# A decoder layer on one core: what opens TensorE's work, and who computes the last layer norm's mean and variance

## What is computed

```python
x = layernorm(x + self_attention(x))             # 16 heads of 64, causal
x = layernorm(x + cross_attention(x, ctx, mask)) # 16 heads of 8, with biases
# feed-forward: 8 experts of width 256, two of them weighted per token
for e in range(8):
    h = silu(x @ w_gate[e].T) * (x @ w_up[e].T)
    out = out + dense_w[:, e:e + 1] * (h @ w_down[e].T)
x = layernorm(x + out)                           # (y - mean) / sqrt(var + 1e-5)
```

## Time and profile before

| | |
|---|---|
| median of 3 runs | 233.50 us (233.46, 233.50, 234.45) |
| time of the profiled execution | 233.65 us |
| its span, first to last instruction | 231.9 us |
| busy | PE 97%, DVE 83%, ACT 71%, POOL 44% |
| mean granted TensorE clock | 0.999 of full speed |

### The profile page before, as it was taken

How to read it: one execution, slowest core, us unless ns; L and a number is a source line. 1 busy time by engine, 2 the same in 40 slices (tenths; PEclk the granted TensorE clock), 3 DMA queues, 4 the chain that set the end, 5 groups by cost and what they waited for, 6 DMA issues and landing times.

```text
span 231.9 us, 6966 instructions
## 1 busy us (share of the span) xinstructions
PE 224.8 (97%) x2268; PEld 205.0 (88%) x2268; DVE 192.1 (83%) x957; ACT 164.5 (71%) x548; POOL 101.4 (44%) x159
## 2 busy tenths in 40 slices
PE   6999999999999999999999999999999999999991
PEld 6999888997978988978978988789999999999991
DVE  3897798998789889989899879999898565766994
ACT  3768988898999979999989999697475333232000
POOL 4377738797396467922978351231200000100111
PEclk9999999999999999999999999999999999999999
DMA  6998000000000000000002200000000000000000
GB/s 191 366 345 322 8 0 0 4 4 1 0 4 3 0 6 3 0 3 1 1 4 69 114 3 3 3 0 4 0 3 0 1 3 0 4 23 0 25 23 24
DMA packets 7011, 9.10 MB, mean 39 GB/s; under 512 B 1088, under 2 KB 5824, under 8 KB 6592
## 3 DMA queue, kind: packets, MB, share of 16 engines
q1 hardware_dynamic: 4320, 7.09, 8.7%
q10 hardware_dynamic: 2656, 1.57, 2.2%
HBM read 8.14 MB, written 0.52 MB: 37 GB/s over the span
## 4 chain that ended last, share of the span: by engine, by line
PE 96%; issue 1%; POOL 1%; DVE 1%; POOLq 0%
PE bank L1531 13%; PE bank L1429 11%; PE bank L1430 10%; PE bank L1431 10%; PE bank L2028 9%; PE bank L1513 7%; PE bank L1540 7%; PE bank L1581 6%; PE bank L1549 4%; PE bank L1524 3%; PE bank L2038 3%; PE bank L1468 2%; PE bank L1469 2%; PE bank L1470 2%; PE bank L1556 2%; PE bank L1597 1%
## 5 line engine op out<-in xcount | busy, mean ns | idle before, releaser
L515 ACT ACTIVATE probs_s<-masked_s,nmax_s 128x128 f32<-128x128 f32 x128 | 50.1, 401 | 3.6 <-DVE nmax_s L822 2.2
L310 POOL TENSOR_TENSOR probs_s<-probs_s,rec_sum_s 128x512 f32<-128x512 f32 x32 | 33.2, 1042 | 35.4 <-DVE rec_sum_s L829 35.1
L518 ACT ACTIVATE probs_c<-masked_c,nmax_c 128x128 f32<-128x128 f32 x128 | 40.6, 401 | 1.5 <-DVE nmax_c L822 1.4
L576 ACT ACTIVATE silu<-bank 128x256 f32<-128x256 f32 x54 | 20.2, 386 | 30.0 <-PE bank L1431 28.1
L1429 PE MATMUL bank<-ctx_hi,gu_hi 128*128 128x256 f32 x128 | 38.7, 302 | 0.0
L1430 PE MATMUL bank<-ctx_lo,gu_hi 128*128 128x256 f32 x128 | 35.7, 279 | 0.0
L1431 PE MATMUL bank<-ctx_hi,gu_lo 128*128 128x256 f32 x128 | 35.7, 279 | 0.0
L822 DVE CUSTOM_DVE_ANT_0 masked_c<-bank,mask_add 128x128 f32<-128x128 f32 x128 | 29.0, 286 | 4.6 <-PE bank L1524 3.9
L493 POOL TENSOR_TENSOR mv<-mv,minus_half 128x1 f32<-128x1 f32 x8 | 4.3, 549 | 59.9 <-DVE mv L1371 59.9
L822 DVE CUSTOM_DVE_ANT_0 masked_s<-bank,causal 128x128 f32<-128x128 f32 x128 | 29.2, 286 | 1.4 <-PE bank L1513 1.2
L515 ACT ACTIVATION_READ_ACCUMULATOR probs_s<-masked_s,nmax_s 128x1 f32 x128 | 25.4, 198 | 0.0
(11 more groups left out here) (171 smaller groups left out, 587.9 us busy)
## 6 DMA issues: line engine op xcount, KB each, us to landing
raw<-in_gateT SPq DMA_DIRECT2D x1, 1024.0 KB, 9.5
raw<-in_upT SPq DMA_DIRECT2D x1, 1024.0 KB, 12.0
down_sb<-in_down SPq DMA_DIRECT2D x1, 1024.0 KB, 5.1
raw<-in_wvT SPq DMA_DIRECT2D x1, 512.0 KB, 5.6
ctxT_all<-in_ctxT SPq DMA_DIRECT2D x1, 512.0 KB, 6.8
masked_c<-in_mask ACTq DMA_DIRECT2D x1, 512.0 KB, 12.3
wo_sb<-in_woT SPq DMA_DIRECT2D x1, 512.0 KB, 6.8
x_tok<-in_x ACTq DMA_DIRECT2D x1, 512.0 KB, 11.0
```

Source lines behind the costliest of these rows:

```text
L310: pool.tensor_tensor(probs_s[:, g % 2], probs_s[:, g % 2], spread(rec_sum_s[:, 4 * g:4 * g + 4], 2, S), ALU.mult).then_inc(normed[g], 1)
L515: last = act.activation(probs_s[:, g % 2, i, :], masked_s[:, g % 2, i, :], ACT.Exp, scale=-1.0, bias=nmax_s[:, h:h + 1], accum_out=rsum_s[ ...
L518: last = act.activation(probs_c[:, g % 2, i, :], masked_c[:, g % 2, i, :], ACT.Exp, scale=-1.0, bias=nmax_c[:, h:h + 1])
L576: act.activation(silu[:, i % NS, :], g, ACT.Silu).then_inc(silued, 1)
```

## The change

At the opening, GpSimd first clears the tile `x1` and raises `consts`, so that the counts of `consts` move up by one. TensorE waits only for that, multiplies the block of zeros by itself ten times, and waits for both constants only then. At the end, block 0 of the last chunk gets its mean and variance elsewhere: ScalarE sums the block (Copy with an accumulated output), GpSimd turns the sum into minus the mean, ScalarE squares the block with that as bias and sums again, GpSimd divides, adds epsilon and takes the power. The semaphore `bias_ready` is renamed `bias_then_mean` and counts these steps too. VectorE adds up units 11 to 15 with nothing between, and its `normalise_y(LAST, 0)` becomes an addition of minus the mean and a multiplication, after the statistics of block 1.

```diff
-    WARM = 14
+    WARM = 10
...
+        ln_col = sb("ln_col", [P, 4])
...
+            pool.memset(x1[:], 0.0).then_inc(consts, 1)
             pool.memset(ident[:], 0.0)
...
-            pool.wait_ge(consts, 1)
+            pool.wait_ge(consts, 2)
...
-                    pool.wait_ge(var3_done, root_of + 1)
+                    if root_of == LAST * TB:
+                        pool.wait_ge(bias_then_mean, 2)
+                        pool.tensor_scalar(ln_col[:, 1:2], ln_col[:, 0:1], -1.0 / D, None, ALU.mult).then_inc(bias_then_mean, 1)
+                        pool.wait_ge(bias_then_mean, 4)
+                        pool.tensor_scalar(ln_col[:, 3:4], ln_col[:, 2:3], 1.0 / D, EPS, ALU.mult, ALU.add).then_inc(bias_then_mean, 1)
+                        pool.wait_ge(bias_then_mean, 5)
+                        pool.tensor_tensor(mv3[:, 0, 3:4], ln_col[:, 3:4], minus_half[:, 0:1], ALU.pow).then_inc(pow3_done, 1)
+                        continue
+                    pool.wait_ge(var3_done, root_of + (root_of < LAST * TB))
...
+            first = acc[:, LAST % 2, 0, :]
+            act.wait_ge(combined, TB * LAST * E + LAST_UNITS.index((0, E - 1)) + 1)
+            act.activation(res1[:], first, ACT.Copy, accum_out=ln_col[:, 0:1]).then_inc(bias_then_mean, 1)
+            act.wait_ge(bias_then_mean, 3)
+            act.activation(res1[:], first, ACT.Square, bias=ln_col[:, 1:2], accum_out=ln_col[:, 2:3]).then_inc(bias_then_mean, 1)
...
-            sums_of_y(LAST, 0)
-            combine_last(11)
-            mean_of_y(LAST, 0)
-            combine_last(12)
-            variance_of_y(LAST, 0)
-            combine_last(13)
-            combine_last(14)
-            combine_last(15)
+            for u in range(11, 16):
+                combine_last(u)
             sums_of_y(LAST, 1)
-            normalise_y(LAST, 0)
             mean_of_y(LAST, 1)
             variance_of_y(LAST, 1)
+            dve.wait_ge(pow3_done, LAST * TB + 1)
+            wait(dve, stored, 16 * TB * LAST)
+            dve.tensor_scalar(y_out[:, 0, :], acc[:, LAST % 2, 0, :], ln_col[:, 1:2], mv3[:, 0, 3:4],
+                              ALU.add, ALU.mult).then_inc(y_ready, 1)
             normalise_y(LAST, 1)
...
-            pe.wait_ge(consts, 2)
+            pe.wait_ge(consts, 1)
             for i in range(WARM):
-                pe.transpose(OC[:, 0:P], ident[:], ident[:])
+                pe.matmul(OC[:, 0:P], x1[:], x1[:], start=True, stop=True)
+            pe.wait_ge(consts, 3)
```

More of the change, by code:

```diff
@@ L213, in build_decoder @@
             sem(f"ld_{n}") for n in "xT xT_rest wv cwk cwq x ctx mask wo cw gu down".split()]
-        stored, consts, pad_set, mask_set, w_hi_done, w_lo_done, gu_split, x_split, ctx_hi_done, ctx_lo_done, cwk_ready, cwq_ready, bias_step, bias_ready = [
+        stored, consts, pad_set, mask_set, w_hi_done, w_lo_done, gu_split, x_split, ctx_hi_done, ctx_lo_done, cwk_ready, cwq_ready, bias_step, bias_then_mean = [
             sem(n) for n in ("stored consts pad_set mask_set w_hi_done w_lo_done gu_split x_split ctx_hi_done ctx_lo_done cwk_ready cwq_ready "
-                             "bias_step bias_ready").split()]
+                             "bias_step bias_then_mean").split()]
         qk_first, qk_first_a, qk_first_v, kc_proj, kc_evac, kc_lower, cv_proj, cv_evac, k_own_done, cvp_done = [
@@ L351, in key_bias @@
                 bias(pool.tensor_tensor(cb_nat[:], cb_sum[:, :, 0], cb_sum[:, :, 1], ALU.add))
-                pool.tensor_scalar(cb_nat[:, 0:1], cb_nat[:, 0:1], DC ** -0.5, None, ALU.mult).then_inc(bias_ready, 1)
+                pool.tensor_scalar(cb_nat[:, 0:1], cb_nat[:, 0:1], DC ** -0.5, None, ALU.mult).then_inc(bias_then_mean, 1)
             def split_gu(n):
@@ L542, in evac_kc @@
                 act.wait_ge(kc_proj, a + 1)
-                act.wait_ge(bias_ready, 1)
+                act.wait_ge(bias_then_mean, 1)
                 act.activation(k_all[:, 0, 4 * a * S:4 * (a + 1) * S], b[:], ACT.Identity,
@@ L921, in evac_qc @@
                 if n == 0:
-                    dve.wait_ge(bias_ready, 1)
+                    dve.wait_ge(bias_then_mean, 1)
                 dve.tensor_scalar(qc[:, 0], b[:, 0:S], cb_nat[:, 0:1], None, ALU.add).then_inc(cq_evac, 1)
@@ L1041, in _ @@
             lower_w(8)
-            dve.wait_ge(consts, 2)
+            dve.wait_ge(consts, 3)
             group_max("s", 0, 0, Y1)
@@ L1364, in mean_of_y @@
                 b = c * TB + tb
-                dve.wait_ge(stat3_done, b + 1)
+                dve.wait_ge(stat3_done, b + (b < LAST * TB))
                 dve.bn_aggr(mv3[:, tb, 0:2], stat3[:, tb, :]).then_inc(aggr3_done, 1)
@@ L1369, in variance_of_y @@
                 b = c * TB + tb
-                dve.wait_ge(aggr3_done, b + 1)
+                dve.wait_ge(aggr3_done, b + (b < LAST * TB))
                 dve.tensor_scalar(mv3[:, tb, 2:3], mv3[:, tb, 1:2], EPS, None, ALU.add).then_inc(var3_done, 1)
```

## The result

Over 22 runs each, the changed kernel takes 233.25 us (232.96 to 234.06) against 233.84 (233.43 to 234.45) before: ratio 0.9975, 95% interval 0.9967 to 0.9983. It is faster by 0.25%, 0.6 us, with an interval clear of no change, and within the 0.5% that I called no change. The profiled execution took 233.06 us; its span is 231.0 against 231.9.

The account below looks back on a forecast made before the run. TensorE ends the last chain for 96% of the span, so only the opening and what follows its last product count. End -0.67 us, opening 0: median 233.50 becomes 232.83 (-0.3%, "same"), range 232.1 to 233.6.

Parts of the forecast that it names:

- (d): Whole kernel, the forecast itself: 232.83 us, with its own range 232.6 to 233.2; chance 0.71.
- Unit 11 released by its product, unit 15 at 0.06 behind the last one: End, VectorE: without block 0's three steps unit 11 follows its product, and unit 15 starts 0.54 us earlier.
- bn_stats to bn_aggr 0.32, worth 0.13: End, VectorE: with block 0's normalisation moved from between block 1's bn_stats and bn_aggr, 0.45 becomes 0.32, another 0.13 us.
- The later steps keep their distances (0.22, 0.23, 0.58): End, after block 1's bn_aggr: steps to epsilon, power and last normalise stay 0.22, 0.23 and 0.58 us.
- The new chain: End, ScalarE and GpSimd: block 0's statistics, from 225.45 to the power's end at 227.65, hidden with a margin of 0.55 us.
- The opening at 0: Opening, TensorE: zeros from 0.97 end at 5.50 against 5.48; bounds -0.07 and +0.05 us, taken as 0.
- The prediction's own sign against it: Opening: the prediction is wrong if the opening moves first_qk(2) by more than 0.1 us.
- rival (b): Opening: the earlier start brings forward a late clock rise in more runs than profiled; over 0.5% faster, chance 0.15.
- (a): End: gains nothing, as ScalarE and GpSimd take over 0.6 us longer than worked out; 233.4 to 233.6, chance 0.08.
- (c): Opening: slower, the clock stays low or falls back through holes in TensorE's work; 235.4 at 6 us low, chance 0.06.
- My low bound: End: if unit 10 to unit 11 stays at 0.44, unit 15 starts at 227.31 and the gain is 0.52 us.

Follow-up runs that it names:

- e1: The changed kernel with the opening of before (14 transposes of ident), so the change at the end alone; 233.46 us, 0.9981 of before.
- e4: The changed kernel once more, on the same chip as its two parts; 233.36 us, 0.9979 of before.
- e6: The changed kernel with ln_col declared last, so that all other tiles keep the addresses of before; 233.41 us, 0.9986 of before.
- e10: The changed kernel with one more unused tile of 16 bytes a partition in front of ctx_hi; 233.53 us, 0.9992 of before.
- e12: e9 with two unused tiles, 16 bytes a partition where ln_col lies and 48 in front of ctx_hi; 233.46 us, 0.9979 of before.
- e2: The kernel before with the new opening (products of zeros) alone, its end unchanged; 233.95 us, 1.0009 of before.
- e3: The kernel before with block 0's three statistics steps each one unit later, all still on VectorE; 233.37 us, 0.9985 of before.
- e5: The kernel before with only the declaration of ln_col (16 bytes a partition) in its place, unused; executed once, 234.21 us.
- e11: The changed kernel with three copies of 128 columns on ScalarE between block 0's sum and squares; executed once, 232.88 us.
- e9: e3 with the new opening and block 0's normalisation moved as in the change, no tile added; 233.10 us, 0.9966 of before.

## Why the prediction came out

It came out in direction and, for the difference, in size: -0.67 forecast, -0.6 measured. The absolute 232.8 started from the median of three runs, 233.50; over 22 runs before stands at 233.84, and the changed kernel at 233.25, inside the range of 232.1 to 233.6 but just outside the 232.6 to 233.2 of (d). The offset is that of the starting point.

- **Unit 11 released by its product, unit 15 at 0.06 behind the last one**: shown (0.05). Of the 0.54 given to this, 0.53 came (the lag went from 0.58 to 0.05).
- **bn_stats to bn_aggr 0.32, worth 0.13**: the step is shown, 227.65 - 227.32 = 0.33. The move is worth only half of that, by the next point.
- **"The later steps keep their distances (0.22, 0.23, 0.58)"**: wrong. The last is 0.64 in the changed kernel, since GpSimd's power took 0.60 where it had taken 0.55. That is 0.05 of the 0.08 between 0.67 and 0.59. It comes with the move of block 0's normalisation: block 1's power took 0.60 to 0.61 in all nine profiles in which that normalisation starts 0.15 before it (changed, e1, e4, e6 to e10, e12), and 0.55 in the four in which it stands at its old place (before, e2, e3, e5). e11, in which it starts 0.09 before the power, has 0.55 too. So the move gives 0.12 and takes 0.05, which fits the 1.92 of e3 and the 1.86 of e9. Why the power is longer there was not tried.
- **The new chain**: 2.24 us forecast from the end of unit 10's sum (225.41) to the end of the power (227.65), 2.20 measured (225.18 to 227.38). Margin 0.55 forecast, 0.57 measured; e11's delay of 0.60 cost nothing. No table load appeared between silu and the two activations, in the order or in the trace.
- **The opening at 0**: within what the timed runs can tell (e2 against before, e1 against e4). The prediction's own sign against it, a move of `first_qk(2)` by more than 0.1, did appear in the profile (0.13), and 0.10 of it is the weights. What I hadn't foreseen is how far the rise varies between profiles of one opening, and that rival (b)'s mechanism exists: e1's clock rose at 7.8, and its `first_qk(2)` started 0.68 later than in the earlier trace rows. The profiles with zeros have `first_qk(2)` at 6.65 to 7.12, those with 14 transposes at 7.13 to 7.84. Timed, this hardly shows: e2's median is no better than before's. The slowest of 22 runs fell from 234.45 to 234.06. The mean granted clock on record for every timed run gives a hint. Of the 101 runs of the kernel before beside the experiments, 15 have 0.994 or 0.995, and all of these took 234.25 to 234.46; of the other 86, five took so long. The profile of e5, which is before with a tile more, has 0.994, its rise at 7.9 and 234.21. So a late rise, as (b) supposed, may be what makes the slowest seventh of before's runs; it doesn't make the median. In which timed runs the clock rose late isn't on record.
- **Rivals (a) and (c)** did not occur. The end gained 0.59. And in all 14 profiles the clock, once risen, stayed up until TensorE's last product was done, and fell at 229.6 at the earliest.
- **One thing the prediction did not count**: the address shift by `ln_col`, two effects of 0.2 us that cancel. That they did was luck.

One small point stays open in the earlier trace rows: unit 11 came 0.44 behind bn_stats, though its product was done, while in e3 a unit came 0.20 behind the same instruction. My low bound rested on it; in the changed kernel the step from unit 10 to unit 11 is 0.29 (224.83 to 225.12), bound by the product.

## What to carry to other kernels

In an in-order queue, ask of each instruction which waits for the result just before it what stands behind it; here one step of one unit in the order gives the 0.5 us for which the change brought in two more engines. Opening work is worth 0.4 to 0.6 us here; neither what it consists of nor a start 1.3 us earlier shows in the times. Before a gain of a few tenths of a microsecond is ascribed to a change, compare the intervals of instructions that it doesn't touch: a new small tile moved others, and with them the pace of matmuls.

## What was unexpected of the hardware

The pace of TensorE's work depends on where the kernel's tiles lie. 16 bytes more in front of `x_hi` sped up the later projections by 0.16 to 0.21 us over some 1,000 matmuls, mostly in those of L1429 to L1431, and slowed the feed-forward's gate and up products by 0.2 us; 32 bytes in front of `ctx_hi` made that 0.56, and 64 bytes 0.40. The effect in the feed-forward repeats to 0.01 us over the seven profiles with `ln_col` in its first place and no other new tile, that in the projections to 0.05 us. Which tile and which engine's access it is was not tried.

Shifts that arise in the opening (the clock's rise, a weight transfer) last to the end. Against before, e3's TensorE was 0.83 us late at its 60th product (11 us), 1.02 at its 160th (22 us) and 0.98 at the last; e1's 0.53, 0.49 and 0.51. In e3 the clock had risen early, at 5.5, and a weight transfer came late, at 7.70. Its chain of waits:

```profile
2.09 5.61 DMA raw<-in_wqT
```

This is where most of the spread of about 1 us between runs of one kernel can arise; only the profiled executions show it, and for the timed runs it is argued.
